# Attention and channel mixing for 32 sequences on one core: one exp instruction for two key-major score products

## The reference

```python
x = x + attn(layernorm(x))     # q, k = rope(x Wq'), rope(x Wk'); v = x Wv'
                               # softmax(q k' / 4) v per head, then Wu and bu
x = x + ffn(layernorm(x))      # xr, xk: mixtures of a token and the one before it
                               # sigmoid(xr W_r) * (square(relu(xk W_k)) W_v)
```

## Time and profile before

| | |
|---|---|
| time, median of 3 runs | 2344.21 us (2334.54 to 2346.26) |
| profiled execution, its time | 2337.8 us |
| its span, from first to last instruction | 2336.0 us |
| TensorE busy (matmul) | 2151.0 us, 92% |
| VectorE busy | 2072.3 us, 89% |
| ScalarE busy | 1647.4 us, 71% |
| GpSimd busy | 1405.7 us, 60% |
| mean granted clock of TensorE | 0.971 of full speed |

### The profile page before, as it was taken

One profiled execution on the slowest core, in us unless ns is written; L12 is line 12 of the kernel. 1 busy time (PEld: TensorE's weight loads), 2 busy tenths in 40 slices (PEclk: granted clock), 3 DMA queues, 4 the chain that ended last, 5 costly groups with the idle time before them and its releaser, 6 DMA issues.

```text
span 2336.0 us, 39602 instructions
## 1 busy us (share of the span) xinstructions
PE 2151.0 (92%) x13084; PEld 1103.6 (47%) x13084; DVE 2072.3 (89%) x3982; ACT 1647.4 (71%) x3137; POOL 1405.7 (60%) x1184
## 2 busy tenths in 40 slices
PE   5999999999999999999999999999999999999984
PEld 4444444544444444444444444444444444444443
DVE  5889989999999999999999999998999999998872
ACT  2467777777777777777777777777777777777662
POOL 5337756566766566765556776655676655676234
PEclk7789999999999999999999999999999999999987
DMA  6434445544445544345553444554444555434410
GB/s 153 108 92 103 103 93 125 128 103 100 96 89 127 126 114 100 92 98 112 126 126 99 98 103 89 126 127 104 98 97 90 126 126 111 99 97 93 97 29 23
DMA packets 133466, 242.09 MB, mean 104 GB/s; under 512 B 24848, under 2 KB 79760, under 8 KB 120976
## 3 DMA queue, kind: packets, MB, share of 16 engines
q1 hardware_dynamic: 133264, 239.56, 45.6%
HBM read 136.71 MB, written 83.89 MB: 94 GB/s over the span
## 4 chain that ended last, share of the span: by engine, by line
PE 35%; DVE 24%; POOL 17%; issue 11%; ACT 5%; SPq 5%; DMA 3%; DVEq 0%; POOLq 0%; ACTq 0%
PE d_ps L956 15%; DVE mx L695 12%; PE st_ps L894 10%; PE pv_ps L926 5%; POOL f_lo L469 3%; PE s_ps L912 3%; DVE sums L719 2%; SPq L318 2%; POOL rope_t L419 2%; POOL parts L413 2%; ACT probs L654 2%; SPq L329 2%; PE d_ps L950 2%; DMA q_st<-mparts 2%; POOL r_lo L455 2%
## 5 line engine op out<-in xcount | busy, mean ns | idle before, releaser
L654 ACT ACTIVATE probs<-st_ps 128x512 f32<-128x512 f32 x2048 | 1152.9, 595 | 515.3 <-PE st_ps L894 492.1
L695 DVE TENSOR_REDUCE mx<-s_ps 128x1 f32<-128x512 f32 x2048 | 1328.7, 677 | 175.7 <-PE s_ps L912 172.6
L894 PE MATMUL st_ps<-q_st,k_st 50*128 50x512 f32 x2048 | 810.7, 462 | 53.4 <-ACT probs L654 35.8
L912 PE MATMUL s_ps<-k_st,q_st 48*128 48x512 f32 x2048 | 831.3, 470 | 18.2 <-DMA k_st<-parts_scratch 7.9
L894 PEld LDWEIGHTS st_ps<-q_st,k_st 50*128 50x128 f32 x2048 | 327.4, 187 | 682.8 <-ACT probs L654 454.1
L926 PE MATMUL pv_ps<-probs,v_ext 128*32 128x512 f32 x4096 | 555.5, 615 | 0.2 <-ACT probs L654 0.2
L477 POOL TENSOR_TENSOR rs<-ve,mhalf 128x2 f32<-128x2 f32 x128 | 89.7, 700 | 497.3 <-DVE mean L761 497.3
L912 PEld LDWEIGHTS s_ps<-k_st,q_st 48*128 48x128 f32 x2048 | 332.7, 188 | 58.3 <-DVE mx L695 48.9
L469 POOL TENSOR_TENSOR f_lo<-yn,f_hi 128x512 fp32r<-128x512 f32 x128 | 174.3, 1380 | 88.5 <-ACT f_hi L622 88.5
L462 POOL TENSOR_TENSOR f_lo<-attnT,f_hi 128x512 fp32r<-128x512 f32 x64 | 87.2, 1363 | 181.0 <-ACT f_hi L610 181.0
L926 PEld LDWEIGHTS pv_ps<-probs,v_ext 128*32 128x32 f32 x4096 | 81.5, 109 | 180.7 <-issue 178.7
(11 more groups left out here) (116 smaller groups left out, 3961.8 us busy)
## 6 DMA issues: line engine op xcount, KB each, us to landing
parts_scratch<-parts SPq DMA_DIRECT2D x64, 1024.0 KB, 4.7
q_st<-parts_scratch SPq DMA_DIRECT2D x128, 256.0 KB, 5.4
k_st<-parts_scratch SPq DMA_DIRECT2D x128, 256.0 KB, 6.2
xn<-in_L_attn_x_dram SPq DMA_DIRECT2D x32, 512.0 KB, 9.2
q_st<-parts_scratch SPq DMA_DIRECT2D x128, 128.0 KB, 6.9
k_st<-parts_scratch SPq DMA_DIRECT2D x128, 128.0 KB, 7.1
attnT<-attn SPq DMA_DIRECT2D x512, 32.0 KB, 2.0
y<-in_L_attn_x_dram SPq DMA_DIRECT2D x32, 512.0 KB, 6.5
```

Source lines behind the costliest of these rows:

```text
L654: nc.scalar.activation(probs[:, u % SLOTS, j, :], st_ps[:, n % 2, :], ACT.Exp, scale=float(D) ** -0.5).then_inc(exp_done, 1)
L695: nc.vector.tensor_reduce(mx[:, col:col + 1], s_ps[:, ring_bank(n), :], AX.X, ALU.max).then_inc(max_done, 1)
L894: nc.tensor.matmul(st_ps[:, n % 2, :], k_st[par][row:row + SROWS + MROWS, slot, c * P:(c + 1) * P], q_st[par][row:row + SROWS + MROWS, slo ...
L912: nc.tensor.matmul(s_ps[:, ring_bank(n), :], q_st[at][row:row + SROWS, slot, qc * P:(qc + 1) * P], k_st[at][row:row + SROWS, slot, :], sta ...
```

## The change

ScalarE makes one exp for products 0 and 1 of a unit and one for 2 and 3. Each reads both banks of `st_ps` (128 x 1024) and writes two heads of `probs`, and it counts two on `exp_done`. It waits for the second of the two products. The entries of `extras` keep their places after (u, j), so those after an even j now come ahead of the pair's exp.

```diff
                     for j in range(GH):
-                        if b.active():
+                        if b.active() and j % 2 == 1:
                             n = GH * u + j
                             act.wait_ge(st_ready, b.count(SCORES, n + 1))
-                            if j == 0:
+                            if j == 1:
                                 if b.has(UNITS, u - SLOTS + 1):
                                     act.wait_ge(pv_done, b.count(UNITS, u - SLOTS + 1))
-                            nc.scalar.activation(probs[:, u % SLOTS, j, :], st_ps[:, n % 2, :], ACT.Exp,
-                                                 scale=float(D) ** -0.5).then_inc(exp_done, 1)
+                            nc.scalar.activation(probs[:, u % SLOTS, j - 1:j + 1, :], st_ps[:, :, :], ACT.Exp,
+                                                 scale=float(D) ** -0.5).then_inc(exp_done, 2)
                         for f, *args in extras.get((u, j), []):
                             f(*args)
```

## The result

The changed kernel took 2368.12 us (median of 4 runs, 2367.05 to 2371.48), the kernel before 2343.53 beside it (4 runs, 2334.54 to 2346.26): ratio 1.0114 [1.0085, 1.0143], **slower by 1.1%**. Forecast were 2403 us and 2.5 to 2.8%. The direction was right and the time lies in the range, but the loss is less than half of the one worked out: profile against profile it is 2367.05 - 2337.8 = 29 us, where the sum said 65.6.

The account below looks back on a forecast made before the run. TensorE (92% busy) and VectorE (89%) were taken to share the bound. Terms summed to 2.05 us a step, 65.6 us over 32 steps, added to 2337.8 us for 2403 us; likeliest range 2365 to 2440, 8 in 10 for 2352 to 2445.

Parts of the forecast that it names:

- units 0 to 3: Stretch until 1060.67 us: four waits, 1.20, and 0.28 in unit 3's transposes, part hidden; counted as +0.55 us a step.
- the base: One step of 68.60 us, from unit 9's first product to the next unit 9's, clock 1.00, on which the sum was made.
- the wait: At each unit's end TensorE waits for the pair's exp: 1.63 us against 1.33 of value products, 0.30 us new per unit.
- unit 9 to R: Unit 9 to dense work R of unit 13: GpSimd's path fixes 18.99 us and idle time absorbs new waits; 0.
- R to 14: From dense work R of unit 13 to unit 14, until 1035.45 us: one full wait, +0.30 us a step.
- 14, 15: Units 14 and 15, until 1043.60 us: two waits and 0.1 for entries behind GpSimd; +0.70 us a step.
- 4 to 6: Units 4 to 6: three waits, 0.90, about half hidden by unit 6's dense work waiting for VectorE's residual; +0.45 us.
- 7: Unit 7: one wait of 0.30 plus 0.2 because the pair's exp stands behind both `yn`; +0.50 us a step.
- 8: Unit 8: product 1's stall of 0.98 us behind product 0 goes, 3.94 us instead of 4.37; -0.45 us with rounding.
- the 0.1 for entries: In units 14 and 15: 0.1 us for ScalarE entries behind GpSimd that the pair's exp now follows.
- VectorE and the others set the pace anyway: Rival for the whole kernel: new waits fall where TensorE waits anyway, time stays at 2338 us; chance 0.10.

Follow-up runs that it names:

- e1: Four single exps a unit as in the kernel before, but ScalarE's other entries in the changed kernel's order; ratio to before 0.9946 [0.993, 0.9961].
- e10: The changed kernel with VectorE's small steps (L755 to L761) moved from after product 1 of unit 9 to after product 3; ratio to before 1.0159.
- e11: Single exps in the changed order (e1), with VectorE's small steps moved from after product 1 of unit 9 to after product 3; ratio to before 0.9968.
- e2: The kernel before, same order and single exps, but both exps of a pair counted on the second, so both banks come free together; ratio 1.0157.
- e3: The kernel before, same order and single exps each counted by itself, but the first of a pair also waits for the second product; ratio 1.0054.
- e12: The kernel before with only VectorE's small steps (L755 to L761) moved from after product 1 of unit 9 to after product 3; ratio to before 0.999.
- e13: The kernel before with four more matmuls of 128x512 put ahead of R of unit 13, whose result R overwrites; ratio to before 0.9991.

## Why the prediction was right in direction and wrong in size

The mechanism is confirmed: a pair starts with its second product, frees both banks at its end, and is covered within a unit but not at its end. What failed are terms of the sum, above all two: the hiding in units 0 to 3, whose waits were put at +0.55 us and cost nothing in the mean (item 2), and the base, one undisturbed step taken for all, so that the 0.31 us a step that before loses behind R, and the changed kernel doesn't, stood at nothing (item 4). The other misses are smaller: the length of the wait, and unit 9 to R (items 1 and 3). In means over 24 steps of the middle, us a step; the last column is free of the hold:

| piece | summed | measured | of it order (e1 - before) | of it pairs (after - e1) | pairs (e10 - e11) |
|---|---|---|---|---|---|
| unit 9 to R | 0 | -0.25 | -0.10 | -0.15 | +0.07 |
| R to 14 | +0.30 | -0.06 | -0.31 | +0.25 | +0.25 |
| 14, 15 | +0.70 | +0.43 | 0 | +0.43 | +0.43 |
| 0 to 3 | +0.55 | -0.02 | -0.04 | +0.02 | +0.09 |
| 4 to 6 | +0.45 | +0.35 | 0 | +0.35 | +0.35 |
| 7 | +0.50 | +0.35 | +0.15 | +0.20 | +0.19 |
| 8 | -0.45 | -0.58 | -0.16 | -0.42 | -0.43 |
| step | +2.05 | +0.22 | -0.46 | +0.68 | +0.96 |

1. **The wait: 0.30 summed, 0.24 measured.** The pair took 1.021 us, not 1.04. The Trainium skill, "ScalarE: Activation LUTs", section "What ACT_TABLE_LOAD costs", gives 0.833 ns an element; 512 of them on top of the measured 595 ns made the estimate of 1.022 us, and the trace agrees with it (1.021). The start of 0.53 us after the product had been read off a first product of unit 9; after a second product it is 0.49. Over the eight to nine unit ends that reach the end of a step this is about 0.5 us of the 1.8 missed. In units 14 and 15 the 0.1 for entries didn't show either.

2. **Units 0 to 3: +0.55 summed, nothing measured.** The hiding there was only half counted. Before, in unit 2, product 1 stood 0.53 us behind product 0 (median of 24 steps), waiting for an exp behind ScalarE's entries, and VectorE set the start of product 2. Now product 1 follows at 0.34, and four waits of 0.24 fall into time that TensorE spent waiting for others: unit by unit the change is +0.09, +0.01, -0.02 and +0.03 us, and the four take 17.21 us in a typical step, 17.09 before (medians).

3. **Unit 9 to R: 0 summed, -0.25 measured.** Right that GpSimd's path hides four waits there; the idle time before R fell from 1.12 to 0.65 us as foreseen. But the path itself got shorter. VectorE's `yn`, for which `f_hi` waits, comes behind the small steps, and one of these, L760, took less time; GpSimd and VectorE in the earlier trace rows's step of before,

```profile
1015.27 1.04 POOL L448 TENSOR_TENSOR xrT<-ynT 128x512 f32<-128x512 f32 x1
1015.73 0.60 DVE L760 TENSOR_SCALAR ve<-mv 128x2 f32<-128x2 f32 x1
```

and at the same place after:

```profile
1029.19 1.03 POOL L448 TENSOR_TENSOR xrT<-ynT 128x512 f32<-128x512 f32 x1
1030.00 0.25 DVE L760 TENSOR_SCALAR ve<-mv 128x2 f32<-128x2 f32 x1
```

L760 ends 0.02 to 0.03 us after GpSimd's operation in both. So the hold has a smaller form, which lasted some 0.35 us longer in all 24 steps of before: L760 starts 2.6 to 2.7 us behind unit 9's first product in both kernels, but GpSimd's operation ends 3.22 us behind it before and 2.90 after (medians). That makes 18.77 us instead of 18.99 from unit 9 to R in a typical step. e1 has it too (2.93 and 18.72 us), so it comes with the order; the -0.15 of the pairs is the long form, which struck 11 steps of e1 and 6 of the changed kernel. With the hold out of the way the piece is +0.07, near the 0 that was summed. It is luck, the same instructions met at another instant, and not something that the change does by design.

4. **R to 14: the wait of 0.25 is there; what repaid it wasn't in the sum.** Before lost 1.5 us of clock behind R in 5 of 24 steps. The account of the kernel before and the prediction read the clock as 1.00 in the steady part from the page's slices, which are too coarse to show such a loss, and took one step of 68.60 us for all: the mean of 24 is 69.35. The changed kernel has no such loss, and a sum made on an undisturbed step can't see that. Why it has none is open: e1 has none either, but nor have e2 and e3 in the order of before.

5. **Unit 8** gained as summed: product 1 stands 0.35 us behind product 0, not 0.98. e1 shows who earned it: the order brings product 1 forward (0.39 us) but pushes the end of unit 8 back (from product 3 to the next product 2.02 us, before 1.61), and 7 and 8 together take 8.29 us, as before; the pairs take 8.07.

6. **The ends: 7 x 2.05 = 14 summed, 22.5 measured.** With fewer sequences in flight little hides a wait; sixteen of 0.24 make 3.8 us a step, and the ends lost 3.2. Beside that the clock of the last stretch is 0.92 of full, before 0.96. The windows bound its share. Length times the lost part of the clock is 14.4 and 10.8 us in the two ends of before, 17.2 and 22.7 after, so at most about 15 of the 22.5 us are clock by these rounded values, and at least 7 us, some 1 us a step, are wait. e1's ends are 1.7 us longer than before's (its span is 9.6 us shorter, its middle 11.3), so nearly all of it belongs to the pairs.

So the span's +29.2 us is -9.6 for the order and +38.8 for the pairs, of which 17.8 in the middle (1739.74 - 1721.90) and 21.0 at the ends. With the hold out of the way, e10 against e11, the pairs cost 50.3 in the profiled runs, 23.8 and 26.5, and 45 by the medians.

That the time lies in the range is partly luck: it is 3 us above the lower end, and the ends lost 8 us more than summed, while the middle lost 6.5 us in 25 steps instead of 51.

Of the signs named beforehand, these came: 1.02 us a pair, 1.57 us at unit ends with ScalarE as releaser, 1.94 within a unit, 0.35 in unit 8, R's idle time at 0.65, VectorE idler. Two didn't: the step is 69.3 to 69.6 us, not 70 to 71, and ScalarE's busy time fell by 62 us, not 100, though its exps' own fell by 108: single exps had overlapped with the entries between them.

Of the rivals, "VectorE and the others set the pace anyway" was closest in the middle of the run, and wrong: with the order held fixed the pairs cost 0.68 us a step there, 0.95 without holds. The rule of "Perfetto Trace Analysis" in the Trainium skill, section "Optimizing Scalar/DVE Operations", that where an engine isn't saturated but makes bubbles on others smaller instructions may finish work sooner, agrees with the runs: single exps in the same order are faster (0.9968 against 1.0159), and 1024 starts saved were worth nothing.

The version to keep is e1, single exps in the new order: 0.9946 [0.993, 0.9961] of before. The gain is small and in part unexplained.

## What to carry to other kernels

An instruction that reads both halves of a double buffer turns it into a single one: its price is start delay plus duration plus release, less the work that the producer has between its last write and its next, at each place apart. A diff that merges instructions also reorders the others around them; run the order by itself before judging the merge. And sum against the mean of many steps, not one: the lumps that a typical step lacks, of either sign, were here as large as the effect.

## What the runs showed of the hardware that was not expected

- The granted clock fell behind R in 5 of 24 steps of before (6 in e12) after 1.12 us of idle time, and in none of e1, e3 or e11 after the same idle time; with that time filled it didn't fall there either (e13). What decides stays open.
- A VectorE instruction on 128x2 elements that was under way together with a GpSimd tensor operation on 128x512 lasted until 0.02 to 0.03 us after that operation's end: L760 took 0.60 us before and 0.25 after, by how long ahead of that end it began (0.17 in e10 to e12, where it was moved). L761 starts within 0.03 us of the start of GpSimd's second operation and took 1.08 us in some steps, to that operation's end, and 0.16 in the others; which one isn't explained. The long form moved a step by 0.9 us.
- Value products of two heads in a row took about what those of four take (busy 944.7 us against 555.5).
